# Attention a: VectorE's steps written out, one-hot and normalisation moved to GpSimd, a shorter verdict, and an opening on two DMA queues

## The reference, cut to what matters

```python
topk = max(1, int(Tx * 0.3))                 # 76
scores = einsum('bhid,bhjd->bhij', q, k) * scale
topk_scores, indices = top_k(scores, topk)
masked = full_like(scores, -inf).at[..., indices].set(topk_scores)
out = einsum('bhij,bhjd->bhid', softmax(masked), v)
```

## Time and profile before

| | us |
|---|---|
| median of three runs | 5192.93 |
| the profiled execution, its own time | 5187.39 |
| its span | 5185.5 |

### The profile page before, as it was taken

The page is one execution under the profiler, slowest core; times in us unless marked ns, Lnnn a source line. Parts: engine busy times, 40 slices in busy tenths (PEclk is TensorE's granted clock), DMA queues, the critical chain, the costliest instruction groups (busy, mean ns, idle before and its releaser), DMA issues. The chain is left out here.

```text
span 5185.5 us, 120998 instructions
## 1 busy us (share of the span) xinstructions
PE 4522.9 (87%) x34302; PEld 3170.4 (61%) x34302; DVE 4012.6 (77%) x14195; ACT 3174.4 (61%) x10274; POOL 2564.9 (49%) x3089
## 2 busy tenths in 40 slices
PE   4688888788878878887999999899999998999998
PEld 3344444444434444443788888666666666888887
DVE  4899999999989999997788888555555555888886
ACT  4688888888868888885222222477676774222222
POOL 1567667676657676676444444211111112444444
PEclk8566667666656676666999999999999999999999
DMA  3000000000000000000444444100000001444444
GB/s 76 10 11 13 13 10 13 10 13 14 10 10 14 10 13 10 14 14 4 83 82 84 86 87 87 25 11 11 11 11 11 11 11 40 87 87 86 82 82 98
DMA packets 359400, 188.83 MB, mean 36 GB/s; under 512 B 190736, under 2 KB 347824, under 8 KB 358960
## 3 DMA queue, kind: packets, MB, share of 16 engines
q1 hardware_dynamic: 358960, 183.74, 17.5%
HBM read 147.24 MB, written 11.01 MB: 31 GB/s over the span
## 5 line engine op out<-in xcount | busy, mean ns | idle before, releaser
L874 ACT ACTIVATE junk<-SS,nt 128x256 bf16<-128x256 f32 x3072 | 1517.0, 501 | 157.1 <-POOL nt L478 107.4
L495 POOL TENSOR_SCALAR gone<-SS,mid 128x256 bf16<-128x256 f32 x1024 | 1178.6, 1167 | 561.2 <-DVEq L1067 453.2
L1241 POOL TENSOR_TENSOR f_hid<-f_g_m,f_cbs 128x256 f32<-128x256 f32 x1024 | 743.7, 726 | 849.9 <-DVE f_g_m L1486 666.4
L1341 ACT ACTIVATE f_th<-bank 128x256 f32<-128x256 f32 x1088 | 416.9, 383 | 1146.0 <-PE bank L1272 1146.0
L1271 PE MATMUL bank<-f_xTf,wgT 128*128 128x256 f32 x2176 | 693.2, 400 | 51.4 <-DVE f_g_m L1486 36.0
L1887 DVE TENSOR_REDUCE nmxb<-bank 128x2 f32<-128x512 f32 x512 | 329.4, 685 | 475.9 <-PE bank L1659 475.9
L1272 PE MATMUL bank<-f_xTf,wuT 128*128 128x256 f32 x2176 | 652.3, 382 | 0.0
L1303 PEld LDWEIGHTS bank<-wdT,f_hid 128*128 128x128 f32 x4096 | 602.4, 192 | 65.0 <-POOL f_hid L1241 11.6
L1303 PE MATMUL bank<-wdT,f_hid 128*128 128x128 f32 x4096 | 630.4, 277 | 9.5 <-POOL f_hid L1241 9.3
L652 PE MATMUL bank<-k,q 32*128 32x256 f32 x2048 | 422.9, 548 | 218.9 <-DVE SS L988 216.7
L874 ACT ACTIVATION_READ_ACCUMULATOR junk<-SS,nt 128x1 f32 x3072 | 596.6, 194 | 0.0
(11 more groups left out here) (229 smaller groups left out, 7644.8 us busy)
## 6 DMA issues: line engine op xcount, KB each, us to landing
f_cbs<-f_shares SPq DMA_DIRECT2D x512, 256.0 KB, 5.8
q4x<-q SPq DMA_DIRECT2D x64, 256.0 KB, 2.3
k4x<-k SPq DMA_DIRECT2D x64, 128.0 KB, 2.1
qrow<-q_rows SPq DMA_DIRECT2D x512, 8.0 KB
q_rows<-qTb SPq DMA_DIRECT2D x32, 128.0 KB, 1.7
out_dram<-xres SPq DMA_DIRECT2D x4, 1024.0 KB, 9.4
q4x<-max_rows SPq DMA_DIRECT2D x128, 4.0 KB
f_shares<-f_combT SPq DMA_DIRECT2D x64, 32.0 KB, 1.5
```

The source lines that it names most:

```text
L495: last = pool.tensor_scalar(gone[:, h % 4, i, :], SS[:, (u - lag) % 4, c, :], mid[:, (u - lag) % 4, 0, c:c + 1], 0.0, ALU.subtract, ALU.min)
L874: nc.scalar.activation(junk[:, c % 2, :], SS[:, uu % 4, c, :], ACT.Sign, bias=bias(c), accum_out=acc[:, k, uu % 4, c:c + 1]).then_inc(s["s ...
L1241: pool.tensor_tensor(hid[:, e % NBUF, :], g_m[:, e % NBUF, :], cbs[:, par, e, :], ALU.mult).then_inc(s["hid"], 1)
```

## The change

VectorE's program for attention a has no hardware loop any more: its 69 steps stand one after the other, while the other engines keep their loop. The one-hot row is made by GpSimd, as a difference and a comparison with zero, right behind `upper`, in two buffers; VectorE waits for a new semaphore `hot`. The two operations of `normed` become two GpSimd operations of 256 elements at the end of `front`, with a wait for `m0c`. The verdict loses two small operations; GpSimd's `hi_t` waits for the sum (`picked`) and no longer for `failed`. The add of the output rows (L1106) is one operation of 256 instead of two of 128. In the opening ScalarE's queue issues nine of the small loads; PE waits for 24 loads; the two biases that it does not need, the expert weights and the rest of x are issued by SP at the head of attention a, ahead of its loads of `px`.

```diff
+        def written_out(eng, step):
+            for t in range(-1, GROUPS + 4):
+                step(t, t // 2, t % 4)
...
-                    pool.tensor_tensor(rstd[:, :], vareps[:, :], half_pow[:, :], ALU.pow).then_inc(s["rstd"], 1)
+                    own.link(pool.tensor_tensor(rstd[:, :], vareps[:, :], half_pow[:, :], ALU.pow))
+                    wait(pool, s["m0c"], 0 if isinstance(b, int) and b == 0 else m0_before(b - 1, "xT"))
+                    pool.sem_inc(s["pgate"], 1)
+                    own.link(pool.tensor_tensor(xn[:, :, :], xpair(b), mv[:, :, 0:1].to_broadcast([P, HALVES, D]), ALU.subtract))
+                    pool.tensor_tensor(xn[:, :, :], xn[:, :, :], rstd[:, :].unsqueeze(2).to_broadcast([P, HALVES, D]), ALU.mult).then_inc(s["xn"], 1)
...
-                        wait(pool, s["failed"], t - 2)
+                        wait(pool, s["picked"], t - 2)
...
                         pool.sem_inc(s["upper"], 1)
+                        own.link(pool.tensor_tensor(oh[:, u % 2, :, :], iota[:, :, :], kk[:, u % 2, :].unsqueeze(2).to_broadcast([P, GT, 15]),
+                                                    ALU.subtract))
+                        pool.tensor_scalar(oh[:, u % 2, :, :], oh[:, u % 2, :, :], 0.0, None, ALU.is_equal).then_inc(s["hot"], 1)
                     if even and ahead:
                         front(bb + 1)
...
-                        hot = own.mark(V.tensor_tensor(oh[:, :, :], iota[:, :, :], kk[:, y, :].unsqueeze(2).to_broadcast([P, GT, 15]), ALU.is_equal))
+                        wait(dve, s["hot"], t - 1)
...
-                        above = own.mark(V.tensor_tensor(fine[:, z2, :], L[:, y, :, 0], hi_t[:, y, :], ALU.is_lt))
+                        level = own.mark(V.tensor_tensor(tmp[:, :], L[:, y, :, 0], hi_t[:, y, :], ALU.is_ge))
...
-                        apart = own.mark(V.tensor_tensor(nxt[:, :], mid[:, z2, 1, :], mid[:, z2, 0, :], ALU.is_lt))
-                        positive = own.mark(V.scalar_tensor_tensor(tmp[:, :], mid[:, z2, 0, :], 1.0e-6, nxt[:, :], ALU.is_gt, ALU.mult))
-                        both = own.mark(V.tensor_tensor(fine[:, z2, :], fine[:, z2, :], tmp[:, :], ALU.mult))
-                        V.tensor_scalar(fail[:, 0:GT], fine[:, z2, :], 0.0, 0.0, ALU.is_equal, ALU.add, accum_out=fail[:, GT:GT + 1]).then_inc(s["failed"], 1)
+                        apart = own.mark(V.scalar_tensor_tensor(nxt[:, :], mid[:, z2, 1, :], 1.0e-6, mid[:, z2, 0, :], ALU.max, ALU.is_ge))
+                        V.scalar_tensor_tensor(fail[:, 0:GT], nxt[:, :], 0.0, tmp[:, :], ALU.add, ALU.max, accum_out=fail[:, GT:GT + 1]).then_inc(s["failed"], 1)
...
-                        if h == 1 and even and front:
-                            normed(bb + 1)
...
-                schedule(dve, step)
+                written_out(dve, step)
```

The opening, cut to its order:

```diff
             @block.sync
-                for i, w in enumerate((W_qkv[0:P, :], W_qkv[P:2 * P, :], W_qkv[2 * P:3 * P, :], W_out,
-                                       Wq, Wk, Wv, Wp, sh_gate, sh_up, sh_down)):
+                for i, w in enumerate((W_qkv[0:P, :], W_qkv[P:2 * P, :], W_qkv[2 * P:3 * P, :], W_out)):
...
             @block.tensor
-                pe.wait_ge(s_w, 16 * 26)
+                pe.wait_ge(s_w, 16 * 24)
...
             @block.scalar
+                for i, w in enumerate((Wq, Wk, Wv, Wp, sh_gate, sh_up, sh_down)):
+                    nc.scalar.dma_start(nat[:, 4 + i, :], w).then_inc(s_w, 16)
+                nc.scalar.dma_start(gnat[:, :], gate_w).then_inc(s_w, 16)
+                nc.scalar.dma_start(pnat[:, :, :], pos.rearrange("(k p) d -> p k d", p=P)).then_inc(s_w, 16)
```

More of the change, by code:

```diff
@@ L148, in build @@
         s_xr = sem("s_xr")
+        s_b = sem("s_b")
         s_stage = sem("s_stage")
@@ L346, in build @@
         s = sems("a", "mv rstd xn m0 m0c m1 m1c var sig scores evac signs u0 u1 u2 thr failed flag okay "
-                      "copied turned biased qrows spgate out pused pt pv on own aown pown slow oc gate pgate upper vput ini wt wtc")
+                      "copied turned biased qrows spgate out pused pt pv on own aown pown slow oc gate pgate upper vput ini wt wtc hot picked")
         max_rows = nc.dram_tensor("max_rows", (P, GT), f32, kind="Internal").ap()
@@ L429, in _, with xpair @@
                 own = Own(pool, s["pown"])
+                def xpair(b):
+                    if isinstance(b, int):
+                        return xres[:, b * HALVES:(b + 1) * HALVES, :]
+                    return xres[:, bass.ds(b * HALVES, HALVES), :]
                 def front(b):
@@ L541, in _ @@
             def _(sp):
+                sp.dma_start(bo[:, :], b_out.rearrange("(a n) -> a n", a=1).to_broadcast([P, D])).then_inc(s_b, 16)
+                sp.dma_start(gbias[:, :], gate_bias.rearrange("(a n) -> a n", a=1).to_broadcast([P, NE])).then_inc(s_b, 16)
+                sp.dma_start(stage[:, 0], w_gate.rearrange("e i h -> (e i) h").rearrange("(k p) h -> p k h", p=P)).then_inc(s_stage, 16)
+                sp.dma_start(stage[:, 1], w_up.rearrange("e i h -> (e i) h").rearrange("(k p) h -> p k h", p=P)).then_inc(s_stage, 16)
+                sp.dma_start(stage[:, 2].rearrange("h k (e i) -> h (k e) i", e=2), w_down.rearrange("e h i -> h e i")).then_inc(s_stage, 16)
+                n = (BATCH - 2) * HALVES // 3
+                for c in range(3):
+                    k = slice(2 * HALVES + c * n, 2 * HALVES + (c + 1) * n)
+                    sp.dma_start(xres[:, k, :], x_dram[:, k, :]).then_inc(s_xr, 16)
+                sp.wait_ge(s_b, 32)
                 sp.wait_ge(s_pext, 1)
@@ L1021, in picks @@
                         y = (u + 1) % 2
-                        hot = own.mark(V.tensor_tensor(oh[:, :, :], iota[:, :, :], kk[:, y, :].unsqueeze(2).to_broadcast([P, GT, 15]), ALU.is_equal))
-                        yield
-                        own.need(own.n)
-                        first = own.mark(V.tensor_tensor(pick[:, 0, :, :], oh[:, :, :], L[:, y, :, 0:15], ALU.mult))
-                        second = own.mark(V.tensor_tensor(pick[:, 1, :, :], oh[:, :, :], L[:, y, :, 1:16], ALU.mult))
@@ L1027, in picks @@
-                        above = own.mark(V.tensor_tensor(fine[:, z2, :], L[:, y, :, 0], hi_t[:, y, :], ALU.is_lt))
+                        wait(dve, s["hot"], t - 1)
+                        if own.n:
+                            own.need(own.n)
+                        first = own.mark(V.tensor_tensor(pick[:, 0, :, :], oh[:, y, :, :], L[:, y, :, 0:15], ALU.mult))
+                        second = own.mark(V.tensor_tensor(pick[:, 1, :, :], oh[:, y, :, :], L[:, y, :, 1:16], ALU.mult))
+                        level = own.mark(V.tensor_tensor(tmp[:, :], L[:, y, :, 0], hi_t[:, y, :], ALU.is_ge))
@@ L1104, in step @@
                             wait(dve, s["biased"], bb - 1)
-                            for i in range(HALVES):
-                                n = V.tensor_tensor(xrow(bb - 2, i), xrow(bb - 2, i), M1[:, i * P:(i + 1) * P], ALU.add)
-                            n.then_inc(s["m1c"], 1)
+                            rows = xres[:, (bb - 2) * HALVES:(bb - 1) * HALVES, :] if isinstance(bb, int) else xres[:, bass.ds((bb - 2) * HALVES, HALVES), :]
+                            V.tensor_tensor(rows, rows, M1[:, 0:T].rearrange("p (i d) -> p i d", i=HALVES), ALU.add).then_inc(s["m1c"], 1)
                         if h >= 1:
```

33 lines of the change are left out of this document (6 added, 27 removed).

## The result

The changed kernel took 5360.99 us (median of four runs, 5355.64 to 5361.19) against 5195.61 us for the kernel before on the same chip. The ratio is 1.0318, 95% interval 1.0295 to 1.0342. The forecast was 5158 with 0.55 on faster. It was wrong, and the time lies above its range.

What follows compares the result with a forecast made beforehand. The prediction took a chain through GpSimd (twice), ScalarE and VectorE in attention a to bound the nearly full VectorE's kernel. From 5187.4 us it subtracted 12 for the body and 17 for the opening, giving 5158, range 5055 to 5205.

Steps and rivals of the forecast that it cites:

- rival for the slower side: VectorE's checks of flags: 64 jumps over repair code at up to 2.7 us each, 173 us, giving 5331; chance 0.08.
- The pair of steps, 71.1 us: Attention a: new pair 69.4 + 2.3 - 0.41 - 0.16 = 71.1 us against a mean of 71.7, gaining 17 us over 28 pairs.
- What was counted on GpSimd: Even step, ahead of the guess: difference 0.68, comparison 0.70, norm 1.45, links 0.2, together 3.0 us more.
- 0.95 us of cover: ScalarE's earlier waiting for PE ahead of flags, taken to absorb that much of the 3.0 us later guess, leaving 2.1.
- Its pair of 69.4: Attention a in the earlier trace: a pair without the loop's return, VectorE busy 66.2 us, used as the base.
- the check against the mean of 71.7: Attention a: 69.4 plus half a return, 1.9 us, gives 71.3, taken as close to the mean pair.
- The loop's return, -3.75 us in two pairs: VectorE's fetch wait at the loop's return in attention a: 3.75 us go, once in two pairs.
- What leaves VectorE: Attention a: one-hot 0.41 and verdict 0.16 us a step, norm 0.52 a pair; 1.7 us a pair in all.
- The opening, 17 us: Before attention a: PE starts near 12.8 us instead of 17.79, and the stage begins 17 us earlier, bounds 12 and 18.
- Half a chain, pair 68.1: Attention a rival: ScalarE regains the delay, so the later guess does not reach okay; gain 122 us, 5066; chance 0.22.
- GpSimd dearer: Attention a rival: four GpSimd operations at 1.17 us and shared ports; pair 73.0, 5217 at worst, 5200 middle; chance 0.12.
- The sum's own range: Whole kernel: comparison cost moving 16 us each way, with the opening's bounds, gives 5135 to 5185 around 5158.

Runs made afterwards that it cites:

- opening_verdict: The changed kernel with one-hot and norm back on VectorE, plus padding that keeps the expert loops from stalling; 5103.63 us, ratio 0.9828.
- masks_late: opening_verdict with GpSimd's masks of heads 4 and 5 moved into the next step; 5136.9 us, ratio 0.9899.
- delay_guess: opening_verdict with two idle GpSimd operations in even steps where the moved norm's would stand, the norm staying on VectorE; 5170.75 us, ratio 0.9957.
- before_wo: The kernel before with only VectorE's steps of attention a written out, expert loops kept from stalling; 5155.47 us, ratio 0.9938.
- hot_pool: opening_verdict with only the one-hot moved to GpSimd; 5104.97 us, ratio 0.9828.
- hot_slack: hot_pool with the one-hot's two GpSimd operations placed behind the first move instead of in front of it; 5099.58 us, ratio 0.9822.
- norm_pool: opening_verdict with only the norm moved to GpSimd; 5169.77 us, ratio 0.9962.
- norm_fill3: norm_fill1 with the same two PE matmuls run three times, so four extra matmuls a pair; 5159.41 us, ratio 0.993.
- norm_fill1: norm_pool with two of PE's max-row matmuls moved ahead of the second projection of q in even steps; 5156.59 us, ratio 0.9919.

## Why the prediction was wrong, point by point

**Its unspoken step: nothing changes outside attention a and the opening.** This is the first step that failed, and the larger one. The sum has no term for the other layers; the second expert layer, with its code unchanged, took 147.9 us more, and this alone takes the kernel from 5211 to 5361. Its rival for the slower side had the right resource, VectorE's instruction fetch, at the wrong place: the 64 jumps over the repair code cost nothing to be seen (2 "issue" waits at MAX8, 5.5 us, in opening_verdict, as in the earlier trace rows), while a loop 2,000 us later came to stand at another place. Its 173 us are near the 148 measured, by chance.

**The pair of steps, 71.1 us.** Measured 73.1. What was counted on GpSimd nearly held: difference 0.59 us (0.68 forecast), comparison 0.88 (0.70), norm 0.61 each (0.72); from the end of `kk` to the first guess GpSimd took 9.6 us and not 6.9, so 2.7 more (3.0 forecast). `flags` came 21.6 us behind the statistics and not 20.0 (medians), 1.6 later (2.1 forecast), and the gap at the check was 1.5 us on the mean where 2 to 3 were forecast. The step that failed here is that ScalarE's delay, less 0.95 us of cover, passes to `flags` and `okay` and nowhere else. It also went to ScalarE's copy of q; PE stood for it, ran the stretch behind it at 0.50 to 0.64 in all 27 pairs, and VectorE stood up to 4.0 us for its scores, 91.5 us in all and not 26.6. How the wait and the clock hang together is open, as masks_late shows; the delay itself brings the longer pair (delay_guess). The forecast had read the earlier trace rows for busy time only. Its pair of 69.4 was read wrong twice. The window of the earlier trace rows is 1.1 us longer than the pair it covers, whose statistics stand at 1081.1 and 1149.4, 68.3 us apart. And this pair was one of those at full clock (1.00 in the window from 25 us on), while two kinds of pairs stood in the trace. With half a return the true pair gives 70.2 and not 71.3, so the check against the mean of 71.7 held only by the long window. Two windows of the kernel before, 25 to 31 us behind the statistics at 719.0 (a pair of 77.0) and at 796.0 (one of 68.3):

```profile
744.00:750.00 6.00, 6.00 (x27) 2.84 (x26) 6.00 (x24) 3.76 (x13) 3.29 (x7) 0.50 0.01 1
...
821.00:827.00 6.00, 6.00 (x49) 3.46 (x48) 6.00 (x26) 6.00 (x21) 5.42 (x8) 1.00 0.00 0
```

**The loop's return, -3.75 us in two pairs.** Right in kind, too large in size: 14 returns of 3.75 us make 52, and before_wo gained 30. As many of its pairs as before, 10 of 27, ran at the lower clock. In the changed kernel, where every pair does, nothing was left of it (attention a 2456.7 us with the loop, 2459.3 without).

**What leaves VectorE.** "0.16 us a step" for the verdict, 10 us in all, was too small: it was worth some 30 with the add. In the table 20 pairs and not 16 kept the clock, 13 us of it; both kinds of pairs are also 0.6 to 0.7 us shorter. The one-hot, 0.41 us a step, was worth nothing (hot_pool), since `zt` took 20 ns more each of 32 times a pair.

**The opening, 17 us.** 20.3 measured, above its bound of 18. PE's transposes began at 9.92 us, not 12.8. SP's last small load was issued 5.3 us earlier (at 6.89, before at 12.16), as counted; but it landed 3.0 us after its issue and not 5.6, where the forecast had kept the old landing time. GpSimd's longer work for the first batch did not show in the start, which is taken at the statistics.

**Half a chain, pair 68.1.** This rival describes opening_verdict and hot_slack, at 68.3 to 68.5 us, but not the change. The one that came nearest for attention a was *GpSimd dearer*, 73.0, for another reason, so by luck.

**The sum's own range.** "5135 to 5185" does not come out of its terms: 16 and 1 us below 5158 and 16 and 5 above give 5141 to 5179. It changes nothing.

## What to carry to other kernels

Compare the stages first, the untouched ones too: when an engine's program grows or shrinks, every later loop on that engine begins at another place, and from some places a loop stalls in each round (here one of 272 instructions); "issue" waits once a round and more packets in the queue of instructions give it away, and a few instructions of padding, 32 here, cured it. In a pipeline where PE waits often, read PE's granted clock in short windows pair by pair before counting a chain: 1.8 us of delay on GpSimd cost 3.2 in a pair here, with the clock of a stretch at 0.50 in place of 1.00. An operation ahead of a value that another engine waits for can cost far more than its length, or nothing: the guess 1.0 us later was free (hot_pool), 1.6 us later cost 66 us (norm_pool). So try the move with idle operations first, which prices the place alone.

## What was not expected of the hardware

- 32 instructions that do nothing, in VectorE's program, changed the time by 150 us of 5361; 106 of them made the kernel before 2.6% slower.
- Four extra matmuls a pair on PE made attention a 37 us faster (norm_fill3 against norm_fill1), with 14 pairs above 0.85 in place of one.
- The pairs of one run fall into two kinds, 68.5 and 71.8 us, with PE's granted clock at 1.00 or 0.50 over the same 6 us of work.
- VectorE's operation that writes `zt` took 524 ns on the mean after and 494 before. It goes with the one-hot on GpSimd: 517 in hot_pool, 496 in norm_pool, 497 in opening_verdict. By what way was not tried.
- The same wait of PE, 2.29 us, stands in pairs that keep the clock and in pairs that lose it (masks_late).
